# Softmax attention's front: q and k biases by TensorE, their move by ScalarE, pad clearing later, the root's table earlier

## The chip, the cores and the metric

The program runs on one core of one Trainium2 chip. The metric is device time of one execution in microseconds, taken as the median of several runs. Five engines work from queues of their own and meet at semaphores: TensorE (PE; its weight loads are listed as PEld), VectorE (DVE), ScalarE (ACT), GpSimd (POOL) and SyncE (SP), which issues most DMAs. TensorE's clock has two levels here, 2.4 GHz (granted clock 1.0) and 1.2 GHz (granted clock 0.5).

## What is computed

Eight blocks in a row over x of shape 2 x 1024 x 128, each of the form x = x + block(layernorm(x)). The change lies in the fifth, a transformer layer with softmax attention. Its front is this part of the reference (H = 16 heads of 8 columns, the eight biases and affine rows drawn at random, so none of them is zero):

```python
def _L1_attn_a_ref(x, Wq, bq, Wk, bk, Wv, bv, Wo, bo, W1, b1, W2, b2, g1, beta1, g2, beta2):
    B, S, d = x.shape
    H, hd = (NUM_HEADS, HEAD_DIM)
    x_norm = layer_norm(x, g1, beta1)
    q = (x_norm @ Wq + bq).reshape(B, S, H, hd).transpose(0, 2, 1, 3)
    k = (x_norm @ Wk + bk).reshape(B, S, H, hd).transpose(0, 2, 1, 3)
    v = (x_norm @ Wv + bv).reshape(B, S, H, hd).transpose(0, 2, 1, 3)
    q = apply_rope(q)
    k = apply_rope(k)
    q = q * (1.0 / jnp.sqrt(jnp.float32(hd)))
    scores = jnp.einsum('bhqd,bhkd->bhqk', q, k)
    attn = jax.nn.softmax(scores, axis=-1)
    ...
x = x + _L1_attn_a_ref(_layernorm(x, axis=-1), ...)
```

## The kernel before

The order on every engine is written out by hand; there is no scheduler. Each engine has one function per block (`tensor`, `scalar`, `vector`, `gpsimd`, `sync`), and the engines run these functions block after block. The attention block is the class `SoftmaxAttention`. A batch is 8 tiles of 128 tokens (TB = 8); the two batches are called b = 0 and b = 1. PSUM has 8 banks, and a `Turn` is one use of one bank: `claim` waits until the use before it is emptied, `result` waits until it is filled, `moved` until it is emptied.

The front of the block is this, by engine.

- **VectorE** (`vector`, from L2031): for each batch the layer norm (`spread` with the statistics of L166, two roots, which ScalarE takes in `deviation` at L272, and the scaled tokens at L212), then `add_bias` for b = 0 (L2078, eight additions that read q and k from PSUM and write `self.qk`), `rotate` (L2089 to L2094, six passes over 1024 elements), `add_bias` for b = 1, `split` for b = 0 (L2105 to L2114, which writes q and k as sums of two f16 parts), `rotate` and `split` for b = 1, and then the ring of row maxima (`ring_read`, L1634).
- **TensorE** (`tensor`, from L1888): 14 calls of `keep_busy` (L287; one call is one matmul of 384 columns whose result nobody reads, two rows of the profile), then for each batch 8 transposes of normed tokens (L280) and 8 matmuls of 384 columns for q, k and v (L1901). Then `pe.wait_ge(self.pads, 3)`, 4 calls of `keep_busy`, a wait for `high_in`, 3 calls more, waits for `again_in` and `split_in`, and the 64 f16 transposes of b = 0 (`turn_split`, L1723). `loop_tensor` follows: two ring fills (L1614), a wait for the second `again_in` and `split_in`, and then eight rounds of one `keep_busy` call, one `turn_split` of b = 1 and two ring fills. Only after these come the first shift (L1684, L1686) and the main loop.
- **ScalarE** (`scalar`, from L1998): the roots, the tokens' move with the norm's affine part (`move_tokens`, L1963), `clear_pads` (three fills of constants, L1943), `move_values` (L1971, v of each tile after VectorE has read q and k), `clear_value_pads` (four fills and a scaled copy, L1943 and L1955), `move_values` for b = 1, `copy_high` (L1978, L1979, which ends in `again_in`), `move_split` (L1986, PSUM to `qT` and `kT`), and both again for b = 1.

An f32 matmul is two rows in the profile, so 8 matmuls of L1901 stand as x16.

Of the kernel before, what the change touches and what calls it, by code (L numbers as in the profile page):

```python
# [24 lines left out]
ALU = mybir.AluOpType  # L25
ACT = mybir.ActivationFunctionType
# [5 lines left out]
TB = T // B  # L32
# [1440 lines left out]
class SoftmaxAttention:  # L1473
# [144 lines left out]
    def ring_read(self, dve, a):  # L1618
        core, v, slot = self.core, self.core.nc.vector, a % 2
        kind, h, i = self.order[a]  # L1620
        dve.wait_ge(self.ring_in, a + 1)
        if kind == "o":
            view = core.psum[:, 2 * slot:2 * slot + 2, :].rearrange("p a (h r) -> p a h r", r=32)
            den = self.den[:, h % 2, :, :]
            core.vstep(v.reciprocal(den, view[:, :, :, 8]))
            v.tensor_tensor(self.att[:, 2 * h:2 * h + 2, :].rearrange("p a (h d) -> p a h d", d=HD),
                            view[:, :, :, 0:HD], den.unsqueeze(3).to_broadcast([P, 2, H, HD]),
                            ALU.mult).then_inc(self.ring_out, 1)
            return
        b, g, half = self.half_of(h)  # L1630
        qt, j = i
        if a == 0:
            dve.wait_ge(self.pads, 7)
        v.tensor_reduce(self.m4[:, h % 2, qt, 32 * j + 24:32 * j + 25], core.psum[:, 2 * slot:2 * slot + 2, :],  # L1634
                        AX.XY, ALU.max).then_inc(self.ring_out, 1)
# [252 lines left out]
    def tensor(self, pe):  # L1888
        core, w, nc = self.core, self.w, self.core.nc
        ps = core.psum  # L1890
# [3 lines left out]
        for b in range(B):  # L1894
# [3 lines left out]
            for i, turn in enumerate(self.t[b]["qkv"]):  # L1898
                core.claim(pe, turn)
                core.moved(pe, self.t[b]["xT"][i // 4])  # L1900
                nc.tensor.matmul(ps[:, turn.bank, 0:384], core.xnT[:, b, 1 + i * P:1 + (i + 1) * P],  # L1901
                                 w.sa_wqkv[:, :], start=True, stop=True).then_inc(core.filled[turn.bank], 1)
# [48 lines left out]

    def clear_value_pads(self, act):
        zero, one = self.w.consts[:, 0:1], self.w.consts[:, 2:3]
        self.fill(self.m4.rearrange("p a q n -> p (a q n)"), zero)
        self.core.nc.scalar.activation(self.turner, self.w.ident[:, :], ACT.Copy,  # L1955
                                       scale=-1.0 / self.SHIFT).then_inc(self.pads, 1)
# [10 lines left out]
    def move_values(self, act, b):  # L1967
        core = self.core
        for i, turn in enumerate(self.t[b]["qkv"]):
            act.wait_ge(self.qk_out, b * TB + i + 1)  # L1970
# [27 lines left out]
    def scalar(self, act):  # L1998
        core, w, nc = self.core, self.w, self.core.nc
        act.wait_ge(w.sa_in, w.sa_all)  # L2000
# [6 lines left out]
        self.clear_pads(act)  # L2007
        self.move_values(act, 0)
        for g, turn in enumerate(self.t[1]["xT"]):
            self.move_tokens(act, turn, 1, g, 0)  # L2010
        self.clear_value_pads(act)
        self.move_values(act, 1)
        self.copy_high(act, 0)
        self.move_split(act, 0)
        self.copy_high(act, 1)
        self.move_split(act, 1)
# [13 lines left out]
    def vector(self, dve):  # L2030
# [14 lines left out]
        self.add_bias(dve, 0)  # L2045
        self.rotate(dve, 0)
        self.add_bias(dve, 1)
# [26 lines left out]
    def add_bias(self, dve, b):  # L2074
        core, w, v = self.core, self.w, self.core.nc.vector
        for i, turn in enumerate(self.t[b]["qkv"]):
            core.result(dve, turn)
            v.tensor_tensor(self.qk[:, b * TB + i, :], core.psum[:, turn.bank, 0:256], w.sa_bqkv[:, 0:256],  # L2078
                            ALU.add).then_inc(self.qk_out, 1)
        dve.wait_ge(self.qk_out, (b + 1) * TB)  # L2080

    def rotate(self, dve, b):
        core, w, v = self.core, self.w, self.core.nc.vector
        tiles = slice(b * TB, (b + 1) * TB)
        qk = self.qk[:, tiles, :].rearrange("p t (h j e) -> p t h j e", h=2 * H, e=2)
# [10 lines left out]
    def split(self, dve, b):  # L2096
        core, v = self.core, self.core.nc.vector
        tiles = slice(b * TB, (b + 1) * TB)
        if b == 0:
            dve.wait_ge(self.pads, 3)  # L2100
# [446 lines left out]
```

## Time and profile before

| | us |
|---|---|
| median of 3 runs | 976.74 |
| lowest and highest of them | 974.82, 978.44 |
| the profiled execution, its own time | 985.43 |
| span of the profiled execution | 983.5 |
| mean granted TensorE clock in it | 0.933 |
| busy: PE, DVE, ACT, POOL | 861.3, 665.9, 558.2, 198.1 |

All times in the rows below are microseconds from the start of the span, in the profiled execution. The front of the attention block lies between 304 and 373 in it. A row of the timeline gives the start, the busy time of the merged instructions, the engine, the line and the operation, and in brackets the idle time before it with the engine that ended it. "issue" in such a bracket is a wait for which the profile shows no releaser.

### The profile page before, as it was taken

How to read it: one execution, taken by the hardware profiler on the slowest of the kernel's cores; microseconds unless marked ns; L12 is line 12 of the kernel's file. 1: busy time of each engine (PE TensorE's matmuls, PEld its weight loads, DVE VectorE, ACT ScalarE, POOL GpSimd, SP SyncE). 2: the span in 40 equal slices, each digit the busy share in tenths (PEclk: the TensorE clock that was granted, in tenths of full speed). 3: DMA queues.
4: the chain of work that ended last, by engine and by line, in shares of the span. 5: the costliest groups of instructions: out<-in, count | busy, mean ns of one | idle time of the engine just before them, and what ended most of it. 6: DMA issues, size and time to landing. Idle time of an engine off the chain costs nothing.

```text
span 983.5 us, 17217 instructions
## 1 busy us (share of the span) xinstructions
PE 861.3 (88%) x6571; PEld 536.4 (55%) x6571; DVE 665.9 (68%) x1248; ACT 558.2 (57%) x1188; POOL 198.1 (20%) x177
## 2 busy tenths in 40 slices
PE   4889935899988689999999999999996899895894
PEld 2579733599855443333333333333465599594694
DVE  5845882366487988999999888896335354566362
ACT  2442532165534836999989877889754055324152
POOL 2000047255400040000000000000030645104385
PEclk9999957999999968999999999999998799995798
DMA  5740001411120000000000000000060121100434
GB/s 118 201 129 1 2 19 51 123 37 34 42 80 1 1 1 1 2 1 2 1 1 2 2 2 1 1 2 1 2 172 2 61 69 37 43 2 25 125 34 70
DMA packets 54643, 36.86 MB, mean 37 GB/s; under 512 B 9138, under 2 KB 50162, under 8 KB 54546
## 3 DMA queue, kind: packets, MB, share of 16 engines
q1 hardware_dynamic: 47218, 25.98, 9.5%
q0 software_dynamic: 7344, 9.77, 4.3%
q8 instruction: 53, 0.87, 0.4%
q14 instruction: 28, 0.23, 0.1%
HBM read 22.31 MB, written 14.48 MB: 37 GB/s over the span
## 4 chain that ended last, share of the span: by engine, by line
PE 46%; DVE 20%; issue 19%; POOL 8%; DMA 3%; ACT 3%; SPq 1%; POOLq 0%; DVEq 0%; ACTq 0%
PE psum L1705 10%; DVE arena L1634 10%; PE psum L1614 8%; POOL results L1158 5%; PE psum L287 4%; PE psum L1674 3%; POOL results L1169 2%; PE psum L1251 2%; PE psum L402 2%; PE psum L380 2%; POOL slots L1147 2%; PE psum L1686 2%; PE psum L1766 1%; PE psum L1754 1%; PE psum L440 1%
## 5 line engine op out<-in xcount | busy, mean ns | idle before, releaser
L1634 DVE TENSOR_REDUCE arena<-psum 128x1 f32<-128x1024 f32 x256 | 296.8, 1219 | 33.9 <-PE psum L1614 30.8
L1871 ACT ACTIVATE arena<-psum 128x512 f32<-128x512 f32 x512 | 273.0, 599 | 32.9 <-PE psum L1674 24.5
L1294 ACT ACTIVATE arena<-psum,arena 128x128 f32<-128x128 f32 x340 | 96.9, 368 | 123.3 <-PE psum L1261 66.1
L1614 PE MATMUL psum<-arena 32*128 32x512 f16 x512 | 152.5, 388 | 8.3 <-ACT arena L1986 4.5
L1705 PE MATMUL psum<-arena 128*32 128x256 f32 (+1 forms) x1920 | 159.4, 405 | 0.2 <-ACT expert_w L1853 0.2
L1674 PE MATMUL psum<-arena 32*128 32x512 f16 x512 | 150.0, 385 | 0.5 <-ACT arena L1871 0.5
L287 PE MATMUL psum<-la_wqkv,ident 128*128 128x384 f32 x308 | 117.3, 532 | 7.2 <-issue 6.5
L1147 POOL DMA_INDIRECT slots<-xn,arena x64 | 66.3, 1036 | 196.1 <-DVE arena L1371 177.5
L1251 PE MATMUL psum<-arena 128*128 128x128 f32 x680 | 96.2, 286 | 1.4 <-DVE arena L1452 1.3
L287 PEld LDWEIGHTS psum<-la_wqkv,ident 128*128 128x128 f32 x308 | 60.9, 206 | 58.5 <-issue 25.6
L1261 PE MATMUL psum<-arena 128*128 128x128 f32 x680 | 90.4, 276 | 1.0 <-issue 0.7
L1251 PEld LDWEIGHTS psum<-arena 128*128 128x128 f32 x680 | 85.5, 197 | 4.7 <-DVE arena L1452 3.3
L1442 DVE COPY arena<-expert_w 128x1028 f32 x85 | 60.8, 715 | 35.9 <-issue 34.9
L1261 PEld LDWEIGHTS psum<-arena 128*128 128x128 f32 x680 | 83.4, 193 | 1.6 <-issue 1.1
L1614 PEld LDWEIGHTS psum<-arena 32*128 32x128 f16 x512 | 28.4, 93 | 101.8 <-DVE arena L1634 71.3
L1158 POOL DMA_INDIRECT results<-arena x62 | 61.6, 994 | 80.4 <-DVE arena L1457 78.6
L2158 POOL TENSOR_TENSOR x<-x,xn 128x1024 f32<-128x1024 f32 x2 | 4.7, 2358 | 362.6 <-DVE arena L2133 362.6
L1705 PEld LDWEIGHTS psum<-arena 128*32 128x32 f32 x1920 | 38.2, 108 | 71.5 <-issue 62.1
L1674 PEld LDWEIGHTS psum<-arena 32*128 32x128 f16 x512 | 42.3, 91 | 44.9 <-ACT arena L1871 32.3
L1457 DVE TENSOR_SCALAR arena<-psum,arena 128x128 f32<-128x128 f32 x85 | 29.8, 350 | 34.7 <-PE psum L1261 34.4
L1216 PE MATMUL psum<-arena 128*128 128x117 f32 (+1 forms) x128 | 23.4, 368 | 26.0 <-DVE arena L1397 26.0
L1169 POOL DMA_INDIRECT results<-arena x23 | 37.9, 1649 | 20.7 <-DVE arena L1457 14.0
(276 smaller groups left out, 1048.1 us busy)
## 6 DMA issues: line engine op xcount, KB each, us to landing
arena<-slots SPq DMA_DIRECT2D x19, 256.0 KB, 3.1
arena<-results SPq DMA_DIRECT2D x12, 256.0 KB, 4.0
slots<-blank SPq DMA_DIRECT2D x1, 2560.0 KB, 11.5
expert_w<-in_L_attn_b_w_dram SPq DMA_DIRECT2D x1, 2048.0 KB, 8.5
expert_w<-in_L_attn_b_w_dram SPq DMA_DIRECT2D x8, 256.0 KB, 4.8
expert_w<-in_L_ffn_W_dram SPq DMA_DIRECT2D x1, 2048.0 KB, 8.5
expert_w<-in_L_ffn_W_dram SPq DMA_DIRECT2D x8, 256.0 KB, 5.0
results<-arena POOLq DMA_INDIRECT x85
```

The source lines that it names most:

```text
L287: core.nc.tensor.matmul(core.psum[:, bank, 0:3 * D], w.ident[:, :], w.la_wqkv[:, :, :], start=True, stop=True)
L1147: pool.indirect_dma_start(out=self.slots[:, :], out_offset=bass.IndirectOffsetOnAxis(ap=self.slot_int[:, 0, at:at + 1], axis=0), in_=core. ...
L1158: pool.indirect_dma_start(out=self.results[:, :], out_offset=bass.IndirectOffsetOnAxis(ap=self.place_int[:, t:t + 1], axis=0), in_=self.y[ ...
L1251: last = nc.tensor.matmul(ps[:, 2 + p, c * P:(c + 1) * P], own[:, c * P:(c + 1) * P], self.xgT[:, p, :], start=True, stop=True)
L1261: last = nc.tensor.matmul(ps[:, 4 + p, 0:D], self.hT[:, p, c, :], own[:, c * D:(c + 1) * D], start=(c == 0), stop=(c == FC - 1))
L1294: last = nc.scalar.activation(self.hT[:, p, c, :], ps[:, 2 + p, c * P:(c + 1) * P], self.func, bias=own[:, FF + c:FF + c + 1])
L1442: v.tensor_copy(self.own[:, t % self.HELD, :], self.ew.all[:, bass.ds(at, EW)]).then_inc(self.copied, 1)
L1614: last = nc.tensor.matmul(core.psum[:, 2 * slot + keys, :], self.qT[rows, g, q0:q0 + P], self.kT[rows, g, k0:k0 + 512], start=True, stop=True)
L1634: v.tensor_reduce(self.m4[:, h % 2, qt, 32 * j + 24:32 * j + 25], core.psum[:, 2 * slot:2 * slot + 2, :], AX.XY, ALU.max).then_inc(self.ri ...
L1674: self.core.nc.tensor.matmul(self.score_bank(pe, self.tile_of["score", k, j]), self.kT[rows, g, at:at + P], self.qT2[rows, h % 2, :], star ...
L1705: last = nc.tensor.matmul(core.psum[32 * j:32 * j + 32, 7, cols], self.vs[:, b * TB + kt, HG * g + j, :], self.prob[:, k % self.PROBS, j, ...
L1871: nc.scalar.activation(self.prob[:, k % self.PROBS, j, :], core.psum[:, 4 + tile % self.SCORE_BANKS, :], ACT.Exp).then_inc(self.prob_in, 1)
```

## The change

It has four parts.

1. The biases of q and k are no longer added by VectorE. TensorE adds them in PSUM: after each q, k, v matmul comes a second one of one row (`w.ones[0:1, :]` against the first row of `sa_bqkv`) and 256 columns, which accumulates on the first 256 columns of the bank.
2. `add_bias` is gone. ScalarE copies the 256 columns of q and k to `self.qk` in `move_products`, followed by the copy of v as before, tile by tile. `rotate` waits for the 8 copies of its batch.
3. `clear_pads` stands after both calls of `move_products`; `clear_value_pads` is split, and its first part, now `clear_shifts`, stands between `copy_high` and `move_split` of b = 0, its second part between `copy_high` and `move_split` of b = 1. VectorE's first maximum waits for 5 fills where it waited for 7; `split` waits for none.
4. ScalarE takes a root of one element ahead of the wait for the weights at the start of the block.

```diff
@@ ring_read
-            dve.wait_ge(self.pads, 7)
+            dve.wait_ge(self.pads, 5)
@@ tensor
                 nc.tensor.matmul(ps[:, turn.bank, 0:384], core.xnT[:, b, 1 + i * P:1 + (i + 1) * P],
-                                 w.sa_wqkv[:, :], start=True, stop=True).then_inc(core.filled[turn.bank], 1)
+                                 w.sa_wqkv[:, :], start=True, stop=False)
+                nc.tensor.matmul(ps[:, turn.bank, 0:256], w.ones[0:1, :], w.sa_bqkv[0:1, 0:256], start=False,
+                                 stop=True).then_inc(core.filled[turn.bank], 1)
         pe.wait_ge(self.pads, 3)
@@ 
+    def clear_shifts(self, act):
+        self.fill(self.m4.rearrange("p a q n -> p (a q n)"), self.w.consts[:, 0:1])
+        self.core.nc.scalar.activation(self.turner, self.w.ident[:, :], ACT.Copy,
+                                       scale=-1.0 / self.SHIFT).then_inc(self.pads, 1)
+
     def clear_value_pads(self, act):
         zero, one = self.w.consts[:, 0:1], self.w.consts[:, 2:3]
-        self.fill(self.m4.rearrange("p a q n -> p (a q n)"), zero)
-        self.core.nc.scalar.activation(self.turner, self.w.ident[:, :], ACT.Copy,
-                                       scale=-1.0 / self.SHIFT).then_inc(self.pads, 1)
...
-    def move_values(self, act, b):
+    def move_products(self, act, b):
         core = self.core
         for i, turn in enumerate(self.t[b]["qkv"]):
-            act.wait_ge(self.qk_out, b * TB + i + 1)
+            core.result(act, turn)
+            core.nc.scalar.copy(self.qk[:, b * TB + i, :], core.psum[:, turn.bank, 0:256]).then_inc(self.qk_out, 1)
             core.nc.scalar.copy(self.vs[:, b * TB + i, :, 0:HD],
...
     def scalar(self, act):
         core, w, nc = self.core, self.w, self.core.nc
+        nc.scalar.activation(core.ln[:, 7, 0:1], core.eps[:, 0:1], ACT.Sqrt)
         act.wait_ge(w.sa_in, w.sa_all)
...
-        self.clear_pads(act)
-        self.move_values(act, 0)
+        self.move_products(act, 0)
         for g, turn in enumerate(self.t[1]["xT"]):
             self.move_tokens(act, turn, 1, g, 0)
-        self.clear_value_pads(act)
-        self.move_values(act, 1)
+        self.move_products(act, 1)
+        self.clear_pads(act)
         self.copy_high(act, 0)
+        self.clear_shifts(act)
         self.move_split(act, 0)
         self.copy_high(act, 1)
+        self.clear_value_pads(act)
         self.move_split(act, 1)
@@ vector
         dve.wait_ge(w.sa_in, w.sa_all)
-        self.add_bias(dve, 0)
         self.rotate(dve, 0)
-        self.add_bias(dve, 1)
         self.split(dve, 0)
@@ rotate
+        dve.wait_ge(self.qk_out, (b + 1) * TB)
@@ split
-        if b == 0:
-            dve.wait_ge(self.pads, 3)
```

ScalarE's queue of the changed kernel, from the last tile of b = 1 to the split of b = 1 (lines L1945 are fills of `clear_pads` or of `clear_value_pads`, L1983 and L1984 are `copy_high`, L1991 is `move_split`):

```order
L1945 CAST arena<-consts 128x256x8 [waits consts_in]
L1945 CAST arena<-consts 128x256
L1945 CAST arena<-consts 128x256x7
L1983 COPY arena<-arena 128x128x8 [waits sa_high]
L1984 COPY arena<-arena 128x128x8
L1945 COPY arena<-consts 128x1024
L1956 ACTIVATE arena<-ident 128x128
L1991 COPY arena<-psum 128x1024 [waits bank4_filled]
```

The three casts are `clear_pads`; before, they stood ahead of the first copy of v of b = 0, and the next rows of the queue after the copies of b = 1 were the two of `copy_high`.

TensorE's queue of the changed kernel at the end of the products of b = 1:

```order
L1903 MATMUL psum<-sa_bqkv,ones 128x256
L1901 MATMUL psum<-sa_wqkv,xnT 128x384 [waits bank3_emptied]
L1903 MATMUL psum<-sa_bqkv,ones 128x256
L287 MATMUL psum<-la_wqkv,ident 128x384 [waits bank4_emptied,ident16_in,sa_pads]
L287 MATMUL psum<-la_wqkv,ident 128x384 x3
L287 MATMUL psum<-la_wqkv,ident 128x384 [waits sa_high]
L287 MATMUL psum<-la_wqkv,ident 128x384 x2
L1723 MATMUL psum<-ident,arena 128x128 [waits bank4_emptied,sa_split,sa_again]
```

The seven `keep_busy` calls (L287) and their wait for the pads (`sa_pads`) stand where they stood; L1903, the bias matmul, is new, one after each of the 16 of L1901.

## Rows read from the trace of the kernel before

**Rows 1.** The chain of waits, 270 to 372: start, us, what ran.

```profile
306.92 1.28 ACT L272
...
318.42 2.66 DVE expert_w L2078 x8
321.11 1.22 DVE arena L2089
...
328.42 1.20 DVE expert_w L2078 x4
...
341.52 1.24 DVE expert_w L2094
...
347.25 1.62 PE psum L287 x2
```

**Rows 2.** Timeline of VectorE in the front; the columns are told above.

```profile
306.67 0.17 DVE L178 SCALAR_TENSOR_TENSOR ln_small<-ln_small 128x8 f32<-128x8 f32 x1
...
308.54 0.20 DVE L205 RECIPROCAL ln_small<-ln_small 128x8 f32<-128x8 f32 x1 [1.71 <-ACT ln_small L272]
...
314.33 0.17 DVE L178 SCALAR_TENSOR_TENSOR ln_small<-ln_small 128x8 f32<-128x8 f32 x1
...
314.87 0.20 DVE L205 RECIPROCAL ln_small<-ln_small 128x8 f32<-128x8 f32 x1 [0.37 <-ACT ln_small L272]
...
331.19 0.69 DVE L2105 TENSOR_SCALAR arena<-expert_w 128x1024 f16<-128x1024 f32 x1
...
345.92 1.22 DVE L2114 TENSOR_TENSOR arena<-expert_w,arena 128x1024 f16<-128x1024 f32 x1
```

**Rows 3.** Timeline of TensorE, 300 to 348.

```profile
301.32 9.20 PE L287 MATMUL psum<-la_wqkv,ident 128*128 128x384 f32 x28
312.16 1.09 PE L280 MATMUL psum<-ident,arena 128*128 128x128 f32 x8 [1.64 <-DVE arena L212]
313.77 5.40 PE L1901 MATMUL psum<-sa_wqkv,xnT 128*128 128x384 f32 x16 [0.53 <-ACT xnT L1963]
...
320.61 1.06 PE L280 MATMUL psum<-ident,arena 128*128 128x128 f32 x8 [1.44 <-ACT arena L1971]
322.46 7.09 PE L1901 MATMUL psum<-sa_wqkv,xnT 128*128 128x384 f32 x16 [0.78 <-ACT xnT L1963]
329.88 4.87 PE L287 MATMUL psum<-la_wqkv,ident 128*128 128x384 f32 x14 [0.34 <-ACT arena L1971]
335.66 3.73 PE L1723 MATMUL psum<-ident,arena 128*128 128x128 f16 x64 [0.92 <-issue]
343.88 1.04 PE L1614 MATMUL psum<-arena 32*128 32x512 f16 x4 [4.48 <-ACT arena L1986]
```

**Rows 4.** Timeline of ScalarE, 315 to 347.

```profile
315.72 4.60 ACT L1943 CAST arena<-consts 128x2048 f16<-128x2048 f32 x3
320.22 1.41 ACT L1971 COPY arena<-psum 128x128 f32<-128x128 f32 x8
321.47 1.51 ACT L1963 ACTIVATE xnT<-psum,sa_affine 128x512 f32<-128x512 f32 x2
322.81 1.10 ACT L1943 COPY arena<-consts 128x1024 f32<-128x1024 f32 x1
323.74 0.38 ACT L1955 ACTIVATE arena<-ident 128x128 f32<-128x128 f32 x1
323.95 5.62 ACT L1943 COPY arena<-consts 128x256 f32<-128x256 f32 x2
...
336.31 7.43 ACT L1986 COPY arena<-psum 128x1024 f16<-128x1024 f16 x8 [1.79 <-PE psum L1723]
344.11 1.04 ACT L1978 COPY arena<-arena 128x1024 f16<-128x1024 f16 x1 [0.38 <-DVE arena L2106]
345.06 1.04 ACT L1979 COPY arena<-arena 128x1024 f16<-128x1024 f16 x1
```

**Rows 5.** Groups of TensorE by line and shape: busy us, mean ns of one | idle.

```profile
L2310 PE MATMUL psum<-mw_soft,xnT 128*128 128x256 f32 x32 | 7.2, 379 | 0.0
L1754 PE MATMUL psum<-xnT,sa_w 128*128 128x512 f32 x32 | 14.2, 592 | 0.0
L365 PE MATMUL psum<-arena,proj 32*128 32x512 f32 x32 | 4.2, 589 | 0.0
```

**Rows 6.** Timeline of TensorE late in the kernel, 256-column f32 matmuls.

```profile
861.10 3.61 PE L2310 MATMUL psum<-mw_soft,xnT 128*128 128x256 f32 x16
```

**Rows 7.** Stretches: from:to and length, busy PE, PEld, DVE, ACT, POOL, granted clock, DMA share, GB/s.

```profile
319.00:322.40 3.40, 1.24 (x9) 0.85 (x8) 3.37 (x9) 3.40 (x11) 0.00 (x0) 1.00 0.00 0
322.40:325.80 3.40, 3.34 (x6) 1.86 (x7) 3.33 (x3) 3.40 (x5) 0.00 (x0) 0.51 0.00 0
...
339.50:342.90 3.40, 0.00 (x0) 0.00 (x0) 3.33 (x4) 3.40 (x5) 0.00 (x0) 1.00 0.00 0
342.90:347.20 4.30, 1.04 (x4) 0.16 (x4) 4.16 (x12) 2.82 (x3) 0.00 (x0) 0.50 0.00 0
347.20:360.00 12.80, 12.75 (x53) 6.31 (x54) 9.29 (x8) 3.04 (x3) 12.22 (x6) 0.50 0.00 0
360.00:372.00 12.00, 11.24 (x64) 4.70 (x64) 10.91 (x10) 5.06 (x5) 0.00 (x0) 1.00 0.01 1
```

**Rows 8.** Timeline of TensorE in the eight rounds; each L287 row begins a round.

```profile
347.25 1.62 PE L287 MATMUL psum<-la_wqkv,ident 128*128 128x384 f32 x2 [2.33 <-issue]
348.66 1.06 PE L1723 MATMUL psum<-ident,arena 128*128 128x128 f16 x8
349.65 1.04 PE L1614 MATMUL psum<-arena 32*128 32x512 f16 x4
350.62 1.65 PE L287 MATMUL psum<-la_wqkv,ident 128*128 128x384 f32 x2
...
360.54 0.91 PE L287 MATMUL psum<-la_wqkv,ident 128*128 128x384 f32 x2
...
363.52 0.91 PE L287 MATMUL psum<-la_wqkv,ident 128*128 128x384 f32 x2
...
365.79 0.91 PE L287 MATMUL psum<-la_wqkv,ident 128*128 128x384 f32 x2
...
370.66 0.91 PE L287 MATMUL psum<-la_wqkv,ident 128*128 128x384 f32 x2
```

More of the change, by code:

```diff
@@ L2072, in vector @@
                 core.moved(dve, turn)
[L2074 to L2080, printed above, removed]
     def rotate(self, dve, b):
```

## The prediction, made before the changed kernel was run

> **What bounds the kernel now.** I read the chain of waits first, then each engine's timeline of the same stretch. Between 304 and 347 the chain runs almost wholly over VectorE: the root's table load, the additions of L2078, the rotation, the split [rows 1]. VectorE has hardly a gap there, and its last split ends at 345.92 + 1.22 = 347.14 [rows 2]. At 347.25 the chain changes to TensorE, whose queue now starts the eight rounds [rows 1, 8]. Everything later is fixed to that moment: the rounds, the first shift and the main loop are one chain of TensorE, maxima and exponentials. So I ask one thing of the change: **when do the eight rounds begin?** They need three things: VectorE's second split (347.14), ScalarE's second `copy_high` (345.06 + 1.04 = 346.10 [rows 4]), and TensorE itself, which must have done the transposes and the first two ring fills (343.88 + 1.04 = 344.92 [rows 3]). VectorE comes last, with only 1.04 us to ScalarE behind it. That small distance matters most: who takes 6 us of work off VectorE and gives some to ScalarE has a new last one.
>
> **The root's table (part 4).** In batch 0 it is 308.54 - 306.67 = 1.87 us from the variance to the reciprocal, in batch 1, where the table is there already, 314.87 - 314.33 = 0.54 [rows 2]. The load of 1.28 [rows 1] disappears from the chain, and 1.33 us go with it. ScalarE has been idle for 7 us by then, so the early load costs nothing; TensorE's 28 filler rows end at 310.52 and the tokens would now come at 312.16 - 1.33 = 310.83, so they don't get in the way by a small margin of 0.3 [rows 3]. The Trainium skill (ScalarE: Activation LUTs, What ACT_TABLE_LOAD costs) gives about 2.66 us for a switch, a drain of 1.38 included. By that rule the whole sum below would be 1.3 smaller; no row shows the drain, and the difference of the two batches decides.
>
> **The bias matmul (part 1).** No row has a matmul with one row of weights. Two bounds: with 32 rows a 512-column f32 matmul takes as long as with 128 rows (589 against 592 ns [rows 5]), so few rows make nothing cheaper; and 8 matmuls of 256 columns take 3.61 us in a row [rows 6], 0.45 each; two thirds of the 5.40 for eight of 384 columns [rows 3] give the same 3.6. Both hold the tail of the last one, which is paid once, so 3.4 is the lower bound and 3.6 the upper at the full clock, 7.2 at half. A cost of nothing is excluded, since the columns must be streamed. I take 3.5 a batch, the row of the same width and clock. Batch 0: the first product matmul starts at 313.77 - 1.33 = 312.44 and the last ends at 312.44 + 5.40 + 3.5 = 321.3, against 319.2 before. TensorE then transposes batch 1 at once (VectorE's tokens are ready, ScalarE's banks too), where it had waited 1.44 for a copy [rows 3]. From those transposes to the first product it is 322.46 - 320.61 = 1.85. So batch 1's products start at 321.4 + 1.85 = 323.3 and, with TensorE busy ahead of them and thus at the full clock (before, half of them ran at 0.51 [rows 7] and they took 7.09), end at 323.3 + 8.9 = **332.2**, against 329.55.
>
> **The moves (part 2).** ScalarE's copy of 256 columns lies between the 128-column one (1.41 for 8, 0.18 each [rows 4]) and the 1024-column one (0.93 each). At either end ScalarE is through with a tile (0.4 to 1.1) in about the time that TensorE needs for one (8.9 / 8 = 1.1), so only the last tile counts: 0.6 us. Batch 0's q and k are there at 321.3 + 0.4 = 321.7 to 322.0, **where VectorE had begun the rotation at 321.11** [rows 1]. VectorE stands idle from 317 on, for 5 us: that swallows the 1.33 and the first 2.7 of the removed additions. What it gains is the second batch of them, 331.19 - 328.42 = 2.77 [rows 1, 2]. Its second split ends at 347.14 + 0.9 - 2.77 = 345.3, so **on VectorE 1.9 us are won**.
>
> **The pads (part 3) are where I see the loss.** Before, the three casts of `clear_pads` (4.60 [rows 4]) ran under VectorE's layer norm, and TensorE's wait for them was long fulfilled. Now they start when batch 1's last tile is moved, at 332.2 + 0.6 = 332.8, and end at 337.4. Queued behind them on ScalarE: `copy_high` 0, `clear_shifts`, `move_split` 0, `copy_high` 1. Queued behind `pads >= 3` on TensorE: **all seven `keep_busy` calls**, then the transposes that ScalarE's `move_split` waits for. Before, these calls ran while VectorE rotated and cost nothing. Now they are in the chain. Their price: 28 rows took 9.20 at the full clock, so 14 take 4.6 [rows 3]; at half clock 9.2. TensorE has been idle since 332.2, 5.2 us. Before, a stretch with no matmul (339.5 to 342.9) and one with 1.24 of 3.40 were each followed by a granted clock of 0.50 and 0.51; and at 322.4, with matmuls one behind the other, the clock was back after 3.4 us [rows 7]. So I take 3.4 us at half clock (2.6 calls of 1.31) and the other 4.4 calls at 0.66, 2.9: 6.3 in all. They end at 337.45 + 6.3 = 343.7. `copy_high` 0 (2.0) and `clear_shifts` (1.10 + 0.38) lie beside them and end at 341.
>
> Then as before: 336.31 - 335.66 = 0.65 to the first move, 7.43 for the eight moves, and at once 2.0 for `copy_high` 1, for which no VectorE work is missing any more: 343.7 + 0.65 + 7.43 + 2.0 + 0.1 = **353.9**. VectorE is ready at 345.3 and waits. The rest of `clear_value_pads` (two fills, 5.62 [rows 4]) follows at 353.8 and ends by 359.5; the fifth round is the first that needs a bank which ScalarE must move after it, at 353.9 + 4 x 2.5 = 364 or later, so this costs nothing.
>
> **Sum.** The rounds start at 353.9 instead of 347.25: **+6.7 us** on a profiled time of 985.43, which would become 992.1. The runs' median is 976.74, 8.7 lower than the profiled time; I carry the difference over as it is: 983.4. Bounds: the seven calls at the full clock give 342.05 and +5.0; all of them, and the transposes behind them, at half clock (8 x 1.06 [rows 8] for 7.43) give +5.0 + 4.6 + 1.1 = +10.7.
>
> **The clock of the rounds.** Before, the first four rounds took 360.54 - 347.25 = 13.3 us at 0.50 and the later ones less (363.52 - 360.54 = 3.0, 365.79 - 363.52 = 2.3) [rows 7, 8]. A round costs 13.3 / 4 = 3.3 at half clock and (370.66 - 360.54) / 4 = 2.5 at full. TensorE again has a gap ahead of the rounds (transposes end at 347.5, then 3 and 2 us of waiting with two ring fills between), so I expect the same four slow rounds. If there were none, 4 x 0.8 = 3.2 would come back.
>
> **Rivals.**
> - *The clock stays up*, through the seven calls and all the rounds: +5.0 - 3.2 = +1.8, 978.5, not slower by the bound below. The two things it needs are priced apart: the calls at the full clock bring the sum to +5.0, and from the first slow round saved (0.8) on it lies within 0.5%. For it: TensorE works without a gap from 301 to 332, and the calls come late. Against: three gaps of 5.2, 3 and 2 us, where before one of 3.4 with nothing in it was enough [rows 7]. The Trainium skill (TensorE: Matmul & The Clock Gate, Part 1) says that the lower clock is the default and activity releases it, which speaks for the drop; the rows show it too. 0.15.
> - *The clock stays down* through the calls and the transposes: +10.7, 987.4. For it: the four rounds that ran at 0.50 although TensorE was busy for 12.75 of 12.80 us [rows 7]. Against: the quick return at 325.8. 0.15.
> - *VectorE still ends last*: the fills or the calls do not stand in the chain, since the release of TensorE comes earlier than the queue's order says. Then the 1.9 are won: 974.8. Against it stands the order of both queues. 0.07.
> - *The table is loaded again* at the first real root, so that part 4 does nothing: +6.7 + 1.3, 984.7. 0.05.
> - My forecast, +5.0 to +8.5: 0.55. Something not named: 0.03.
>
> **The numbers.** A change of under 0.5% (4.9 us) is about what a measurement here cannot tell from none. Slower: 0.50 of the forecast (0.05 of it falls just under the bound), 0.15 and 0.05, together 0.70. Same: 0.05 + 0.15 + 0.07 = 0.27. Faster: 0.03, the unnamed. The range goes from the clock staying up (+1.8, and 0.5 for the bias matmuls' lower bound and the moves: 978.0) to the clock staying down with one slow round more (+10.7 + 0.8, rounded to 988.5), which leaves out the case of VectorE and parts of the two about the clock, less than 0.2.
>
> **What would show it.** In the profile of the changed kernel: the load ahead of 301 and 0.5 us from variance to reciprocal; the product matmuls of a batch over 8.9 us; VectorE idle about 5 us ahead of the rotation; the fills right behind the last copy, TensorE idle for some 5 us until they end, and L287 with "ACT" as releaser; the wait ahead of the rounds ended by ScalarE's `copy_high`, with VectorE idle for 6 us or more ahead of its first maximum. It is wrong if the L287 rows start before the fills end, or if the rounds begin before 350.

## The result and the profile after

The changed kernel takes 990.72 us (median; 989.97 to 991.56) against 976.74 before. The ratio is 1.0144, with a 95% interval of 1.0118 to 1.0170: **slower by 14 us (11.5 to 16.6)**, where 6.7 were forecast. The time lies above the stated range. The direction was right, and so was the loss forecast for the pads; the size of the whole was half of what came, because the bias matmuls cost more than reckoned. Executions that ran about 2% longer at a lower mean granted clock are left out of the medians here and of all ratios below (in this comparison one of the four of the kernel before, 993.73 us), and of the one profile that caught such an execution, that of `e3_pads_early`, only the front, ahead of 349.7, is used.

The profiled execution took 991.56 us, the one of before had taken 985.43. That difference of 6.1 looks like the forecast's 6.7 and is so by chance: a later profile of the same kernel before took 973.22. The executions differ in how long TensorE runs at half clock, among other things, which is told below.

To compare kernels in spite of that, I measure the **front** alone: from the start of the variance of batch 0 (VectorE, L178) to the first L287 of the eight rounds. Before, it is 347.25 - 306.67 = 40.58 us [rows 2, 8]. In the changed kernel the two ends are these rows (timelines of VectorE and of TensorE: start, us, engine, line, operation; in brackets the idle time ahead and who ended it):

```profile
302.27 0.17 DVE L178 SCALAR_TENSOR_TENSOR ln_small<-ln_small 128x8 f32<-128x8 f32 x1
...
302.87 0.20 DVE L205 RECIPROCAL ln_small<-ln_small 128x8 f32<-128x8 f32 x1 [0.43 <-ACT ln_small L272]
...
320.38 1.23 DVE L2087 TENSOR_TENSOR arena<-expert_w,rope 128x1024 f32<-128x1024 f32 x1 [7.64 <-ACT expert_w L1975]
...
344.08 1.22 DVE L2110 TENSOR_TENSOR arena<-expert_w,arena 128x1024 f16<-128x1024 f32 x1
354.33 2.35 DVE L1634 TENSOR_REDUCE arena<-psum 128x1 f32<-128x1024 f32 x2 [9.03 <-PE psum L1614]
```

```profile
308.09 0.88 PE L1901 MATMUL psum<-sa_wqkv,xnT 128*128 128x384 f32 x2 [0.53 <-ACT xnT L1967]
308.90 0.69 PE L1903 MATMUL psum<-sa_bqkv,ones 1*128 1x256 f32 x2
309.53 0.91 PE L1901 MATMUL psum<-sa_wqkv,xnT 128*128 128x384 f32 x2
...
319.80 1.09 PE L280 MATMUL psum<-ident,arena 128*128 128x128 f32 x8
321.41 0.88 PE L1901 MATMUL psum<-sa_wqkv,xnT 128*128 128x384 f32 x2 [0.53 <-ACT xnT L1967]
...
332.49 0.69 PE L1903 MATMUL psum<-sa_bqkv,ones 1*128 1x256 f32 x2
338.32 6.91 PE L287 MATMUL psum<-la_wqkv,ident 128*128 128x384 f32 x14 [5.13 <-ACT arena L1945]
345.07 3.74 PE L1723 MATMUL psum<-ident,arena 128*128 128x128 f16 x64
...
355.07 1.65 PE L287 MATMUL psum<-la_wqkv,ident 128*128 128x384 f32 x2 [0.74 <-ACT arena L1984]
```

The front is 355.07 - 302.27 = **52.80 us, 12.2 longer**. VectorE is through at 345.30 and then idle for 9.03 us until the first maximum. TensorE waits 5.13 us for the fills (L1945) and then runs the seven filler calls in the chain. That much was forecast. What was not: a tile takes 309.53 - 308.09 = 1.44 us, later 1.47, where 1.1 had been reckoned. ScalarE's queue in the same stretch:

```profile
333.65 4.62 ACT L1945 CAST arena<-consts 128x2048 f16<-128x2048 f32 x3
338.16 1.05 ACT L1983 COPY arena<-arena 128x1024 f16<-128x1024 f16 x1
...
345.71 7.43 ACT L1991 COPY arena<-psum 128x1024 f16<-128x1024 f16 x8 [4.41 <-PE psum L1723]
...
353.90 1.12 ACT L1984 COPY arena<-arena 128x1024 f16<-128x1024 f16 x1
```

### The profile page after: what moved, and what is told of

Same layout as the page of the kernel before. It is cut to its first block, busy times and chain, and to the rows that moved or that the text cites. A ratio compares the mean times of both kernels' runs of the same rounds, so it can differ in the third digit from the quotient of the medians.

```text
span 989.8 us, 17280 instructions
## 1 busy us (share of the span) xinstructions
PE 871.9 (88%) x6603; PEld 539.3 (54%) x6603; DVE 660.5 (67%) x1232; ACT 564.1 (57%) x1205; POOL 199.6 (20%) x177
## 4 chain that ended last, share of the span: by engine, by line
PE 50%; DVE 17%; POOL 13%; issue 10%; ACT 4%; DMA 4%; SPq 1%; POOLq 0%; DVEq 0%; ACTq 0%
DVE arena L1634 10%; PE psum L1705 9%; PE psum L1614 8%; POOL slots L1147 6%; POOL results L1158 5%; PE psum L1674 3%; PE psum L287 3%; POOL results L1169 2%; PE psum L1251 2%; PE psum L402 2%; PE psum L380 2%; PE psum L280 2%; PE psum L1766 1%; PE psum L1686 1%; PE psum L1754 1%
## 5 line engine op out<-in xcount | busy, mean ns | idle before, releaser
L1705 PE MATMUL psum<-arena 128*32 128x256 f32 (+1 forms) x1920 | 159.4, 405 | 0.2 <-ACT expert_w L1853 0.2
L287 PE MATMUL psum<-la_wqkv,ident 128*128 128x384 f32 x308 | 115.4, 527 | 6.2 <-ACT arena L1945 5.1
L287 PEld LDWEIGHTS psum<-la_wqkv,ident 128*128 128x128 f32 x308 | 60.8, 205 | 55.7 <-issue 16.6
L1705 PEld LDWEIGHTS psum<-arena 128*32 128x32 f32 x1920 | 38.2, 108 | 71.7 <-issue 61.8
L1158 POOL DMA_INDIRECT results<-arena x62 | 61.7, 995 | 74.4 <-DVE arena L1457 73.2
L1452 DVE COPY arena<-psum 128x128 f32<-128x128 f32 x85 | 24.0, 283 | 37.0 <-PE psum L1242 37.0
```

The lines of the kernel that those rows point to most:

```text
L287: core.nc.tensor.matmul(core.psum[:, bank, 0:3 * D], w.ident[:, :], w.la_wqkv[:, :, :], start=True, stop=True)
L1158: pool.indirect_dma_start(out=self.results[:, :], out_offset=bass.IndirectOffsetOnAxis(ap=self.place_int[:, t:t + 1], axis=0), in_=self.y[ ...
L1705: last = nc.tensor.matmul(core.psum[32 * j:32 * j + 32, 7, cols], self.vs[:, b * TB + kt, HG * g + j, :], self.prob[:, k % self.PROBS, j, ...
```

## Why a bias matmul costs 0.80 us and not 0.44

The theory that the next experiments test (S): weights with another number of rows are not loaded while a matmul runs. The weight loads (PEld) of the changed kernel, to be laid beside the matmuls above:

```profile
308.90 0.29 PEld L1903 LDWEIGHTS psum<-sa_bqkv,ones 1*128 1x128 f32 x2 [0.54 <-issue]
309.53 0.30 PEld L1901 LDWEIGHTS psum<-sa_wqkv,xnT 128*128 128x128 f32 x2 [0.33 <-issue]
```

Load and matmul of L1903 both start at 308.90, those of L1901 both at 309.53: at every change of kind the load stands bare ahead of its matmul's real work, for about 0.19 us, and there are two changes a tile. The rival (L) has two forms: an accumulation into the same bank waits for the one before it, or a one-row matmul is slow in itself.

**Full rows.** The bias matmul uses 128 rows: the identity against the bias, which `sa_bqkv` holds in every partition. The sums are the same.

```diff
-                nc.tensor.matmul(ps[:, turn.bank, 0:256], w.ones[0:1, :], w.sa_bqkv[0:1, 0:256], start=False,
+                nc.tensor.matmul(ps[:, turn.bank, 0:256], w.ident[:, :], w.sa_bqkv[:, 0:256], start=False,
```

> The changed kernel, but the bias matmul uses all 128 rows: identity as stationary operand against the bias that lies in every partition (the sums are the same). Theory S (switching between a 128-row and a 1-row stationary operand costs TensorE about 0.18 us each way): the pitch of a tile falls from 1.47 to 1.10 us, 8 tiles take 8.8, the front from variance to first round falls from 52.8 to about 47, and the ratio to before from 1.014 to about 1.008. Theory L (a second matmul that adds to the same bank waits for the first one's end, whatever its rows): the pitch stays at 1.47 and nothing moves.

Its timeline, matmuls and then weight loads:

```profile
310.40 0.59 PE L1903 MATMUL psum<-sa_bqkv,ident 128*128 128x256 f32 x2
310.83 0.81 PE L1901 MATMUL psum<-sa_wqkv,xnT 128*128 128x384 f32 x2
311.48 0.59 PE L1903 MATMUL psum<-sa_bqkv,ident 128*128 128x256 f32 x2
```

```profile
310.08 0.51 PEld L1903 LDWEIGHTS psum<-sa_bqkv,ident 128*128 128x128 f32 x2
310.62 0.41 PEld L1901 LDWEIGHTS psum<-sa_wqkv,xnT 128*128 128x128 f32 x2
```

The load of L1903 now starts at 310.08, 0.32 us ahead of its matmul and under the one before. A tile takes 311.91 - 310.83 = 1.08 us, the bias matmul 311.91 - 311.48 = 0.43 of it. The front is 350.88 - 303.86 = 47.0, as expected; the ratio to before 1.0055 (1.0034 to 1.0077), a little lower than the 1.008 expected. The accumulation goes into the same bank as before and its cost is nearly halved, so the first form of L is out. **128 rows of weights are cheaper here than one**, by 0.39 us a tile and 5.8 us of the front.

**Pairs.** The one-row matmuls stay, but two tiles' products come first and then their two bias matmuls, which halves the changes.

```diff
+                if i % 2 == 0:
+                    continue
+                for late in self.t[b]["qkv"][i - 1:i + 1]:
+                    nc.tensor.matmul(ps[:, late.bank, 0:256], w.ones[0:1, :], w.sa_bqkv[0:1, 0:256], start=False,
+                                     stop=True).then_inc(core.filled[late.bank], 1)
```

> The changed kernel, but two tiles' product matmuls stand together and then their two one-row bias matmuls, so there are half as many changes between a 128-row and a 1-row stationary operand. The same matmuls, the same columns. Theory S (each change costs about 0.19 us): a pair takes 2.55 to 2.6 us where two tiles took 2.93, so 8 tiles take 10.3 where they took 11.7, and the front, from variance to first round, falls from 52.8 to about 50. Theory L (the one-row matmul is slow in itself): 2.93 a pair, the front stays.

```profile
308.03 1.13 PE L1906 MATMUL psum<-sa_bqkv,ones 1*128 1x256 f32 x4
309.08 1.56 PE L1901 MATMUL psum<-sa_wqkv,xnT 128*128 128x384 f32 x4
310.57 1.13 PE L1906 MATMUL psum<-sa_bqkv,ones 1*128 1x256 f32 x4
```

A pair takes 310.57 - 308.03 = 2.54 us instead of 2.93: 0.39 saved by two changes fewer, 0.19 each. The front is 350.51 - 300.75 = 49.8. A one-row matmul that is slow in itself, the second form of L, would have left 2.93.

**Thirty-two rows.** Is it the single row? The bias matmul takes 32 rows of ones, so that it adds 32 times the bias of q and k.

```diff
+                nc.tensor.matmul(ps[:, turn.bank, 0:256], w.ones[0:32, :], w.sa_bqkv[0:32, 0:256], start=False,
```

> The changed kernel with 32 rows of ones and of the bias in the bias matmul, so that it adds 32 times the bias of q and k (this part of the computation is changed; the instructions and their sizes are not). Theory S (any change between stationary operands of unlike row counts keeps the weight load from running under the matmul ahead of it): a tile still takes 1.47 us and the front 52.8. The rival (something is special in a single row): 1.10 a tile and a front of 47.

```profile
308.82 0.69 PE L1903 MATMUL psum<-sa_bqkv,ones 32*128 32x256 f32 x2
309.45 0.91 PE L1901 MATMUL psum<-sa_wqkv,xnT 128*128 128x384 f32 x2
310.29 0.69 PE L1903 MATMUL psum<-sa_bqkv,ones 32*128 32x256 f32 x2
```

310.29 - 308.82 = 1.47, the front 355.16 - 302.19 = 53.0. It is the change of the row count, not the number one. Why the array behaves so was not tried further.

No experiment has 64 rows or a change of columns, but the traces of the kernel before do. A first matmul with 64 rows (L2206) behind one with 128 has its load at 149.18 and itself starts at 149.18 in the third profile, with no wait between. And with 128 rows on both sides, but weights of 32 columns ahead (L1705, `128*32`) and of 128 behind, the filler's load is bare too (first profile, matmuls and then the load):

```profile
701.70 0.64 PE L1705 MATMUL psum<-arena 128*32 128x256 f32 x8
702.26 0.91 PE L287 MATMUL psum<-la_wqkv,ident 128*128 128x384 f32 x2
```

```profile
702.26 0.30 PEld L287 LDWEIGHTS psum<-la_wqkv,ident 128*128 128x128 f32 x2 [0.41 <-issue]
```

So what counts seems to be the shape of the weights, rows or columns. These are single rows read from traces, not experiments.

## The pads and the fillers

**Pads early.** `clear_pads` goes back ahead of the first move.

```diff
+        self.clear_pads(act)
         self.move_products(act, 0)
...
         self.move_products(act, 1)
-        self.clear_pads(act)
```

> The changed kernel, but clear_pads stands where it stood, ahead of the first move. Theory P (fills of 4.6 and seven filler calls are in the chain only because the pads come late): the L287 rows start at once behind batch 1's last bias matmul, the front falls by about 7 us from 52.8 to 45.7, ratio to before about 1.007. The rival (ScalarE's queue is the bound, and moving its 4.6 us forward delays the moves of batch 0 and with them VectorE by as much): under 2 us are won.

```profile
335.04 4.78 PE L287 MATMUL psum<-la_wqkv,ident 128*128 128x384 f32 x14
339.66 3.74 PE L1723 MATMUL psum<-ident,arena 128*128 128x128 f16 x64
...
349.66 1.65 PE L287 MATMUL psum<-la_wqkv,ident 128*128 128x384 f32 x2 [0.75 <-ACT arena L1984]
```

The fillers follow the last bias matmul without a gap and, with no gap, run at full clock (4.78 instead of 6.91). The front is 349.66 - 304.20 = 45.5, which is 7.3 less than the changed kernel's; ratio 1.0050 (1.0016 to 1.0083). Theory P holds: 4.6 of fills, 2.1 of slower fillers and some waiting were in the chain only because the pads came late. Moving ScalarE's 4.6 us forward cost VectorE nothing.

**Both.** Full rows and pads early together.

> Both edits together: 128-row bias matmul, clear_pads early. If S and P both hold and add up: the front falls to about 40, like before (40.6); ScalarE's eight moves and second copy_high end last in it; ratio to before 0.997 to 1.003. If the one covers the other: front 43 or more, ratio 1.004 or more.

The front is 343.99 - 304.08 = 39.9: the two losses add (5.8 + 7.3 = 13.1 of 52.8 would be 39.7). Ratio 1.0001 (0.9982 to 1.0021). So these two are the whole loss, and **the rest of the change is worth only 0.7 us of front**. What ends last shows why (VectorE's last split and ScalarE's second `copy_high`):

```profile
341.93 1.23 DVE L2110 TENSOR_TENSOR arena<-expert_w,arena 128x1024 f16<-128x1024 f32 x1
342.82 1.12 ACT L1984 COPY arena<-arena 128x1024 f16<-128x1024 f16 x1
```

VectorE is through 343.16 - 304.08 = 39.1 us after the variance, where it was 40.5 before: 1.4 less, about the table's 1.3. The additions that it no longer does are spent in waiting, 5.35 us ahead of its first rotation. ScalarE ends 0.8 us later, at 343.94, and takes back half of the table's gain.

**No filler.** The seven calls are dropped from the changed kernel.

```diff
-        keep_busy(core, w, pe, self.t[0]["qkT"][0].bank, 4)
         pe.wait_ge(self.high_in, 1)
-        keep_busy(core, w, pe, self.t[0]["qkT"][0].bank, 3)
```

> The changed kernel without the seven filler calls ahead of the first f16 transposes (their results are read by nobody, so nothing that is computed is left out). If they cost what the trace shows, 6.9 us, and nothing hides: TensorE's next wait is for ScalarE's copy_high of batch 0, whose second copy ends at 340.15 in the changed kernel's profile, 1.9 after the fills; the transposes then start near 340.2 where they started at 345.07, the front falls from 52.8 to 48, if the 64 transposes at half clock (8 x 1.06 for 7.43) don't cost 1.0 again; ratio to before 1.014 falls to about 1.010. The rival: the fillers keep the clock up for the rounds; without them the stretch at half clock grows from 6.8 us to over 15 and the ratio stays at 1.014 or more.

```profile
338.98 6.55 PE L1723 MATMUL psum<-ident,arena 128*128 128x128 f16 x64 [7.46 <-ACT arena L1982]
...
349.38 1.65 PE L287 MATMUL psum<-la_wqkv,ident 128*128 128x384 f32 x2 [1.17 <-ACT arena L1982]
```

The front is 349.38 - 300.61 = 48.8, so 4.0 of the fillers' 6.9 us were the price; ScalarE's `copy_high` is the next to be late, and the transposes, partly at half clock, cost 6.55 instead of 3.74. They still lie under ScalarE's moves. Ratio 1.010 (1.006 to 1.014). The rival, a longer stretch at half clock in the rounds, did not show in the profile: two slow rounds, as with the fillers. The single times scatter (980 to 990, as those of pads early do, 978.5 to 992.1), so for the times it stays open.

## The table, and where the forecast's difference of 8.7 us lay

**Table alone**, on the kernel before.

```diff
+        nc.scalar.activation(core.ln[:, 7, 0:1], core.eps[:, 0:1], ACT.Sqrt)
         act.wait_ge(w.sa_in, w.sa_all)
```

> The kernel before with part 4 alone (a root of one element at the start of the block). The front falls from 40.6 to 39.3 us if the whole load of 1.3 comes off the chain, to 37.9 if a drain behind the load went too, and stays at 40.6 if the table is loaded a second time. The time: ratio 0.9985, which the runs may not resolve.

The first round starts at 341.21, the variance at 301.93: 39.28 against 40.58, so 1.3 us as reckoned. No drain shows behind a load: in the first profile of before it ends at 306.92 + 1.28 = 308.20 and the root starts at 308.21. In the times this is too little to see; the profiled execution took 976.22. The Trainium skill (ScalarE: Activation LUTs, What ACT_TABLE_LOAD costs) has 2.66 us for a switch, a drain of 1.38 included; here 1.3 are gained by taking it off the chain.

**The kernel before, profiled again**, twice.

> The kernel before, profiled again, unchanged. The changed kernel's profiled time lay 6.1 us over the first profile of before (991.56 against 985.43), its median 13.1 over. Theory A: the first profile of before is a long one, for a cause ahead of the front (the variance of batch 0 starts at 306.67 in it and at 302.27 in the changed kernel), and not because of the front; a second profile then has a time near 977, the variance near 302, and again about 40.6 us from that variance to the first round. Theory B: the front itself varies from one execution to the next; then that distance is another, by 2 us or more.

> The kernel before once more, for its profile. Both profiles of it so far have TensorE at half clock for 24 us between the first round and the end of the first fills of the main loop, and profiled times of 984.5 and 985.4 at a mean granted clock of 0.932, where its other undisturbed executions have 0.939 to 0.941 and 975 to 979. If the missing 7 us are the clock in the rounds, a profile at 0.94 shows about 7 us at half clock there, a distance of 23.6 instead of 26 to 28 us from the first round to the first shift, and the same 40.6 for the front.

The second profile (984.47 us) has the variance at 303.87 and the first round at 344.43: front 40.56. The third (973.22 us) has 301.07 and 341.68: front 40.61. **Theory B fell: the front is the same to 0.05 us in all three.** This is so although the clock differed inside it: in the third profile batch 1's products took 5.40 us and the seven fillers 6.45, in the first 7.09 and 4.87. VectorE, which ends last in this kernel, covers both. Of theory A half held: the first profile's variance comes 5.6 us later than the third's, but the second profile is as long with only 2.8. The rest of what differs is behind the front. Busy times and granted clock from the first round to the first shift (L1684), in the second profile, in the third, and in the changed kernel (from:to, length, busy PE, PEld, DVE, ACT, POOL, granted clock, DMA share, GB/s):

```profile
344.40:372.40 28.00, 26.87 (x118) 12.25 (x118) 21.48 (x19) 8.10 (x8) 12.23 (x6) 0.65 0.00 1
```

```profile
341.70:365.00 23.30, 21.91 (x119) 9.39 (x120) 21.23 (x19) 8.10 (x8) 12.22 (x6) 0.93 0.00 1
```

```profile
355.00:378.60 23.60, 22.98 (x119) 9.72 (x120) 21.16 (x19) 13.36 (x11) 3.01 (x2) 0.90 0.00 1
```

The same rounds take 28.0 us at a granted clock of 0.65 and 23.3 at 0.93. As expected of it, the third profile has about 7 us at half clock (0.50 from 338.3 to 345.0, half of that ahead of the rounds), and its 23.3 are close to the 23.6 expected. In the profile that the prediction was made from they took 373.27 - 347.25 = 26.0, with four rounds at half clock [rows 7, 8], and another stretch at half clock followed at the start of the main loop. So that profiled time of 985.43 was no neutral base. Of the 12.2 us by which it exceeds the third profile, 5.6 lie ahead of the front, 2.7 are slow rounds, 2.2 the start of the main loop (L1684's first and last lie 309.3 apart in it and 307.0 to 307.1 in the other two profiles and in the changed kernel), and 1.5 come behind it. What causes the 5.6 was not looked into. Against the third profile the changed kernel is 991.56 - 973.22 = 18.3 longer: 12.2 in the front, 1.2 ahead of it, 0.2 in the rounds, and 4.7 behind the main loop, in code that the change does not touch. That stretch, behind the last L1684, is 299.4, 300.9 and 303.3 us in the profiles of the kernel before and 304.1 in the changed kernel's, so most of the 4.7 is within their own spread of 3.9; the rest stays open. What the timed runs show, 14 (11.5 to 16.6), is the front's 12.2 and nothing else that is proven.

## A version that is faster than both

If VectorE waits for TensorE in batch 0, the additions of batch 0 cost it nothing. The mixture keeps them, and gives only batch 1's bias to TensorE, with 128 rows; the pads stay early, the other fills late, the table early.

```diff
-                                 w.sa_wqkv[:, :], start=True, stop=True).then_inc(core.filled[turn.bank], 1)
+                                        w.sa_wqkv[:, :], start=True, stop=(b == 0))
+                if b:
+                    last = nc.tensor.matmul(ps[:, turn.bank, 0:256], w.ident[:, :], w.sa_bqkv[:, 0:256],
+                                            start=False, stop=True)
+                last.then_inc(core.filled[turn.bank], 1)
...
-        self.add_bias(dve, 1)
```

> A mixture: batch 0 as before (VectorE, which waits for TensorE anyway, adds the bias), batch 1's bias by a 128-row matmul (identity against the broadcast bias) and moved by ScalarE, clear_pads early as before, the other fills late and the table ahead as in the change. By the sum from rows: VectorE is through at 36.3 after the variance; TensorE's products of batch 1 end at 23.2, the fillers at 27.9, ScalarE's moves at 36.1 and its second copy_high at 38.1: front 38.2 against 40.6, ratio to before 0.997 to 0.998. If instead batch 1's products run at half clock for 3.4 us, as they do in the kernel before, it is 39.9 and ratio 0.999.

Its front is 342.14 - 302.76 = 39.4, between the two numbers expected: batch 1's first products did run at half clock (granted 0.50 from 317.4 to 320.7), and all of them end by 327.6. Ratio 0.9973 (0.9948 to 0.9998).

Then with four filler calls ahead of the f16 transposes instead of seven:

> The mixture with four filler calls instead of seven ahead of the f16 transposes. In the mixture's profile the products of batch 1 end at 327.6, four calls take 2.6 and end at 330.3, where ScalarE's copy_high of batch 0 has just ended; ScalarE's two late fills end at 331.4 and are then what the moves wait for: front 38.0 instead of 39.4, ratio to before 0.996. If the shorter run of fillers lets the clock stay down longer in the rounds, the ratio is that of the mixture (0.997) or worse.

```profile
325.28 0.59 PE L1904 MATMUL psum<-sa_bqkv,ident 128*128 128x256 f32 x2
325.71 2.74 PE L287 MATMUL psum<-la_wqkv,ident 128*128 128x384 f32 x8
328.44 3.73 PE L1723 MATMUL psum<-ident,arena 128*128 128x128 f16 x64
336.93 1.04 PE L1614 MATMUL psum<-arena 32*128 32x512 f16 x4 [4.76 <-ACT arena L1995]
339.11 1.62 PE L287 MATMUL psum<-la_wqkv,ident 128*128 128x384 f32 x2 [1.14 <-ACT arena L1988]
```

The products ran at full clock in this execution and ended at 325.7; the front is 339.11 - 302.52 = 36.6, 4.0 less than before. It is 1.4 less than expected because of that clock, which the edit did not bring: of the 2.8 us between the fronts of the two mixtures, 1.7 are the earlier end of the products and 1.1 are left for the fillers. Ratio **0.9960 (0.9941 to 0.9978)**, median 971.69 against 975.59 for the kernel before in the same comparison. The intervals of the two mixtures overlap, so the times do not tell them apart. The expectation had ScalarE end last; it is VectorE again, at 339.01 against ScalarE's 338.68:

```profile
337.79 1.22 DVE L2125 TENSOR_TENSOR arena<-expert_w,arena 128x1024 f16<-128x1024 f32 x1
337.55 1.13 ACT L1988 COPY arena<-arena 128x1024 f16<-128x1024 f16 x1
```

| kernel | front, us | ratio to before (95%) |
|---|---|---|
| before | 40.6 | 1.0002 (0.9974 to 1.0030), its copy |
| changed | 52.8 | 1.0144 (1.0118 to 1.0170) |
| full rows | 47.0 | 1.0055 (1.0034 to 1.0077) |
| pads early | 45.5 | 1.0050 (1.0016 to 1.0083) |
| both | 39.9 | 1.0001 (0.9982 to 1.0021) |
| pairs | 49.8 | one execution |
| 32 rows | 53.0 | one execution |
| no filler | 48.8 | 1.0100 (1.0062 to 1.0138) |
| table alone | 39.3 | not resolved |
| mixture | 39.4 | 0.9973 (0.9948 to 0.9998) |
| mixture, four calls | 36.6 | 0.9960 (0.9941 to 0.9978) |

## Why the prediction was right or wrong, step by step

- *VectorE is the bound, the eight rounds are the moment to watch.* Right. Fronts and ratios go together over the kernels of the table that have both, to about 2 us.
- *The table, -1.33.* Right: from variance to first product 308.09 - 302.27 = 5.82 against 313.77 - 306.67 = 7.10, so 1.28, and 1.30 with the table alone.
- *The bias matmul, 3.5 us a batch.* **This is the step that failed.** From the first product of batch 0 to the transposes of batch 1 it took 319.80 - 308.09 = 11.7 us where 9.0 had been reckoned, and batch 1 took 11.8 (321.41 to 333.2) where 8.9 had: 5.6 us over in both together. I had bounded the cost by rows where neighbours have the same number of rows ([rows 5, 6]), and had called a cheaper outcome excluded and a dearer one possible only at half clock. The price is not in the matmul but in the change from one to the other. The kernel before had it in its trace, in every round (weight loads and then matmuls of the sixth round):

```profile
363.52 0.30 PEld L287 LDWEIGHTS psum<-la_wqkv,ident 128*128 128x128 f32 x2 [0.42 <-issue]
363.95 0.10 PEld L1723 LDWEIGHTS psum<-ident,arena 128*128 128x128 f16 x1
...
364.81 0.11 PEld L1614 LDWEIGHTS psum<-arena 32*128 32x128 f16 x2
```

```profile
363.52 0.91 PE L287 MATMUL psum<-la_wqkv,ident 128*128 128x384 f32 x2
364.27 0.61 PE L1723 MATMUL psum<-ident,arena 128*128 128x128 f16 x8
364.82 1.04 PE L1614 MATMUL psum<-arena 32*128 32x512 f16 x4
```

  After the 32-row ring fills the 128-row filler's load and matmul start together, and so do those of the next ring fill, from 128 rows to 32. Between them, where only the type changes (f32 to f16, 128 rows both), the load starts 0.32 us ahead of its matmul. So the type is not the cause.

- *ScalarE's moves hide.* Right: per tile 0.37 and 0.27, with 0.93 of waiting between them.
- *VectorE idle about 5 us ahead of the rotation.* It was 7.64, the bias matmuls' excess of batch 0 on top, and 1.58 more ahead of the second rotation. Because of that its gain of 1.9 went: its last split ends 345.30 - 302.27 = 43.0 after the variance, where it was 347.14 - 306.67 = 40.5. The rival in which VectorE gains 1.9 us had no ground left.
- *Pads late: 4.6 of fills and the fillers in the chain.* Right in mechanism and nearly in size: idle 5.13 (5.2 expected), fillers 6.91 (6.3 expected: they had the half clock for 4.3 us, until 342.6, where 3.4 had been taken). The idle stretch that the prediction gives as 3.4 us was a part of one of 4.48 [rows 3]. The experiment gives 7.3 for the place of the pads.
- *The sum, 6.7.* With 5.6 for the bias matmuls and 0.5 for the fillers on top, and 0.6 off for small terms (the transposes of batch 1 and the steps behind the fillers were shorter than reckoned), it is the measured 12.2. Those 5.6 alone would have put the forecast at 989.
- *The carrying over of 8.7 us between profiled and timed execution.* Harmless, but without ground. The sum was added to the median as if the profile's own excess would stay the same. It lay ahead of the front, in the clock of the rounds and in other stretches of that one execution; that the clock varied, rows had hinted: four rounds at 0.50, four at 1.0, with the same work [rows 7, 8]. It did not move the forecast of the median, but it made the difference of the two profiled times (6.1) mean nothing.
- *The clock of the rounds.* Two slow rounds came instead of four; this was inside what was allowed for. The rivals about the clock, the last one at VectorE and the second table load did not come.
- *The signs in the profile.* The L287 rows began after the fills, with ACT as releaser, and the rounds at 355.07, not before 350. The signs named were there except "8.9 us a batch" (11.7 and 11.8) and, in size, VectorE's idle time.

## What to carry to other kernels

Price an added matmul at the place where it is put: give it the same number of weight rows as its neighbours (here an identity against the bias; filling up with zeros was not run), or group the unlike ones, since here every change cost 0.19 us and one row was dearer than 128. Before a wait is made later, list what is queued behind it on the waiting engine; fillers that were free under another engine's work come into the chain with it. And take a landmark-to-landmark time from the profile, not its total, when the clock has more than one pattern.

## What the runs showed of the hardware

- A weight load did not run under a matmul with another number of rows in any row read here: 0.19 us at each change between 128 rows and 1 or 32 (1.47 us a tile against 1.08; 2.54 us a pair against 2.93).
- With 128 rows on both sides an added 256-column f32 accumulation into the same bank costs 0.43 us; it does not wait for the one before it.
- TensorE can stay at half clock although it is busy nearly all the time: for 12.75 of 12.80 us [rows 7], and for 19.57 of 19.60 in the second profile of before (the row below). The same program's rounds take 23.3, 26.0 or 28.0 us by that. The Trainium skill (TensorE: Matmul & The Clock Gate, Part 1) has sustained activity release the lower clock soon; in these rounds of f16 transposes, 32-row matmuls and fillers it did not always.

```profile
344.40:364.00 19.60, 19.57 (x81) 9.48 (x82) 13.97 (x12) 5.06 (x5) 12.23 (x6) 0.50 0.00 1
```

- After 5.13 us without a matmul the seven filler calls took 6.91 us, with no gap 4.68 to 4.78. After 2.0 us it was once the one and once the other: 6.45 in the third profile of before (idle 2.03), 4.88 with the table alone (idle 2.02).
